# A mixture-of-experts stage on one core: batch entries grouped in blocks of 5 instead of 8, and half of the first weight matrix's split moved from VectorE to ScalarE

## The reference, cut to what matters

```python
for e in range(E):                       # E = 4
    h = gelu(context_c @ ew1[e] + eb1[e])          # 256 -> 1024
    y = h @ ew2[e] + eb2[e]                        # 1024 -> 256
    out = out + w_be[:, e] * mask[e] * y           # w_be is 0 where e is not one of the 2 picked
shared = gelu(context_c @ sw1 + sb1) @ sw2 + sb2
return out + shared
```

## Time and profile before

| What | Value |
|---|---|
| Median of three executions | 2313.76 us |
| Profiled execution: its own time / its span | 2309.97 us / 2308.2 us |
| TensorE matmul busy, share of the span | 2029.4 us (88%) |
| VectorE, ScalarE, GpSimd busy | 1332.8, 975.7, 359.8 us |
| Mean granted TensorE clock | 0.922 of full speed |
| Stretch of the routed units | 361.1 to 607.3 us from the start |

### The profile page before, as it was taken

One profiled execution on the slowest core, in us unless ns is written; L12 is line 12 of the kernel. 1 busy time (PEld: TensorE's weight loads), 2 busy tenths in 40 slices (PEclk: granted clock), 3 DMA queues, 4 the chain that ended last, 5 costly groups with the idle time before them and its releaser, 6 DMA issues. The chain is left out here.

```text
span 2308.2 us, 33746 instructions
## 1 busy us (share of the span) xinstructions
PE 2029.4 (88%) x13199; PEld 1629.9 (71%) x13199; DVE 1332.8 (58%) x2450; ACT 975.7 (42%) x1939; POOL 359.8 (16%) x276
## 2 busy tenths in 40 slices
PE   5699799999899999999999997489966867798798
PEld 3399788888677888888888786378953655456465
DVE  2577457778675446455464313565647457365796
ACT  2144445645453544544544322144433345454332
POOL 2258201323100000000000001057820000000000
PEclk7799899999999999999999998689987966899899
DMA  2555212232016022112000001445561002010000
GB/s 83 189 169 146 53 37 93 91 110 92 20 37 123 25 48 50 36 50 62 23 15 22 26 16 41 154 138 124 130 162 47 2 1 56 19 57 1 0 10 28
DMA packets 110104, 149.39 MB, mean 65 GB/s; under 512 B 6824, under 2 KB 92375, under 8 KB 109560
## 3 DMA queue, kind: packets, MB, share of 16 engines
q1 hardware_dynamic: 98780, 129.07, 19.2%
q0 software_dynamic: 11168, 18.18, 3.9%
HBM read 124.08 MB, written 23.15 MB: 64 GB/s over the span
## 5 line engine op out<-in xcount | busy, mean ns | idle before, releaser
L1828 DVE TENSOR_TENSOR m_h_lo<-m_hf,m_h_hi 128x512 fp32r<-128x512 f32 x256 | 173.7, 690 | 311.0 <-ACT m_hf L1803 307.2
L1800 ACT ACTIVATE m_h_hi<-m_h_ps,m_bT 128x512 fp32r<-128x512 f32 x256 | 177.0, 691 | 366.6 <-PE m_h_ps L396 346.8
L653 POOL DMA_INDIRECT token_sums<-e_y,slot_row x56 | 187.8, 3353 | 97.7 <-DVE e_y L779 83.6
L1803 ACT ACTIVATE m_hf<-m_h_ps,m_bT 128x512 f32<-128x512 f32 x256 | 175.0, 684 | 0.0
L738 ACT ACTIVATE e_h_hi<-e_h_ps,e_b1T 128x320 fp32r<-128x320 f32 (+1 forms) x128 | 78.0, 609 | 169.8 <-PE e_h_ps L396 113.8
L1481 DVE TENSOR_TENSOR c_h_lo<-c_hf,c_h_hi 128x512 fp32r<-128x512 f32 x120 | 91.9, 774 | 89.1 <-ACT c_hf L1431 88.4
L802 DVE TENSOR_TENSOR e_h_lo<-e_hf,e_h_hi 128x320 fp32r<-128x320 f32 (+1 forms) x128 | 72.3, 582 | 110.6 <-ACT e_hf L741 110.6
L1287 POOL TENSOR_TENSOR cT<-cT,c_yg 128x128 f32 x88 | 76.7, 872 | 269.2 <-DVE c_yg L1499 255.5
L1428 ACT ACTIVATE c_h_hi<-c_h_ps,c_b 128x512 fp32r<-128x512 f32 x88 | 62.2, 706 | 106.5 <-PE c_h_ps L396 105.9
L396 PE MATMUL m_y_ps<-m_h_hi,l_w_1hi 128*128 128x512 f32 x256 | 100.3, 392 | 3.4 <-issue 3.4
L396 PE MATMUL m_y_ps<-m_h_hi,l_w_0hi 128*128 128x512 f32 x256 | 99.7, 389 | 1.4 <-ACT m_gT L1814 1.4
(11 more groups left out here) (699 smaller groups left out, 5422.7 us busy)
## 6 DMA issues: line engine op xcount, KB each, us to landing
cT<-in_L_ffn_W_dram SPq DMA_DIRECT2D x30, 1024.0 KB, 5.3
res<-in_L_cond_ew_dram SPq DMA_DIRECT2D x22, 1024.0 KB, 5.1
cT<-in_L_ffn_w_dram SPq DMA_DIRECT2D x16, 1024.0 KB
res<-gates_rows SPq DMA_DIRECT2D x8, 1024.0 KB, 15.0
token_rows<-d_tok SPq DMA_DIRECT2D x2, 2112.0 KB, 10.4
token_sums<-res SPq DMA_DIRECT2D x2, 2048.0 KB, 7.9
res<-token_sums SPq DMA_DIRECT2D x8, 512.0 KB, 5.4
cT<-modulation_rows SPq DMA_DIRECT2D x8, 512.0 KB, 5.7
```

The lines of the kernel that those rows point to most:

```text
L653: pool.indirect_dma_start(out=sums, out_offset=bass.IndirectOffsetOnAxis(ap=st.slot_row[0:r, e, j:j + 1], axis=0), in_=y[0:r, e % 2, j, :] ...
L1800: act.activation(hs[0][:, f, :], h_ps[:, f % HB, :], ACT.Relu, bias=bT[:, at:at + 1])
L1803: act.activation(hf[:, f % HB, :], h_ps[:, f % HB, :], ACT.Relu, bias=bT[:, at:at + 1]).then_inc(act_done, 1)
L1828: dve.tensor_tensor(hs[1][:, f, :], hf[:, f % HB, :], hs[0][:, f, :].bitcast(F32), ALU.subtract).then_inc(h_ready, 1)
```

## The change

The block size `SLOTS` goes from 8 to 5 batch entries. The worst case is then (64 + 4 x 4) // 5 = 16 routed units, each 5 x 64 = 320 columns wide; the shared units keep their 512. So there are 20 units in all. All per-unit operations on `c_x`, `c_h`, `c_y`, `c_xg`, `c_yg` and `c_mix` become 320 wide in routed units, `take` runs for `f` = 0 to 4 alone, and GpSimd makes 5 additions per unit. The high part of W1 is no longer one cast on VectorE after `f` = 2 but two activations on ScalarE (`w1_high`, 1024 elements each), after its gelus of `f` = 1 and `f` = 2, ahead of `take`. VectorE's low halves of W1 wait for them. With 16 instead of 11 routed units the parity at the end changes, so the buffer pairs are swapped for the next phase.

```diff
-SLOTS = BLK // S
+SLOTS = 5
+WT = SLOTS * S
+MOST = (B + SLOTS - 1) // SLOTS
 ROUTED = (PICKED * B + E4 * (SLOTS - 1)) // SLOTS
...
+        wide = lambda u: BLK if u < NB else WT
...
-                        last = split_products(pe, h_ps[:, f % HB, :], [w[:, k, f * P:(f + 1) * P] for w in w1s[i % 2]],
-                                              [x[:, k, :] for x in xs[u % 2]], k == 0, k == KC - 1)
+                        last = split_products(pe, h_ps[:, f % HB, 0:wide(u)], [w[:, k, f * P:(f + 1) * P] for w in w1s[i % 2]],
+                                              [x[:, k, 0:wide(u)] for x in xs[u % 2]], k == 0, k == KC - 1)
...
             def take(u, s):
-                if u >= UNITS or u < NB:
+                if u >= UNITS or u < NB or s >= SLOTS:
                     return
...
+            def w1_high(i, c):
+                act.wait_ge(w1_in, 16 * i)
+                act.activation(w1s[i % 2][0][:, c, :], w1_raw[:, c, :], ACT.Copy).then_inc(w1_hi, 1)
+
...
+                    if u >= NB - 1 and f in (1, 2):
+                        w1_high(u - NB + 2, f - 1)
                     take(u + 1, f)
...
             def prepare(i, f):
-                if f == 2:
-                    dve.wait_ge(w1_in, 16 * i)
-                    dve.tensor_copy(w1s[i % 2][0][:, :, :], w1_raw).then_inc(w1_hi, 1)
                 if f in (3, 4):
-                    dve.wait_ge(w1_hi, i)
+                    dve.wait_ge(w1_hi, 2 * (i - 1) + f - 2)
                     w1_low(i, f - 3)
...
+        w1s, w2s = (pair if ROUTED % 2 == 1 else pair[::-1] for pair in (w1s, w2s))
```

More of the change, by code:

```diff
@@ L1207, in l1_cond_phase @@
         xs = [[sb(f"x_{i}{x}", [P, KC, BLK], F32R) for x in ("hi", "lo")] for i in range(2)]
-        xg = sb("xg", [P, KC, BLK])
+        xg = sb("xg", [P, KC, WT])
         hs = [sb(f"h_{x}", [P, FC, BLK], F32R) for x in ("hi", "lo")]
         hf = sb("hf", [P, HB, BLK])
-        yg, mix = sb("yg", [P, KC, BLK]), sb("mix", [P, SLOTS, S])
+        yg, mix = sb("yg", [P, KC, WT]), sb("mix", [P, SLOTS, S])
         bT, b1 = sb("bT", [P, (E4 + 1) * (FC + KC)]), [sb(f"b1_{i}", [P, FC]) for i in range(2)]
@@ L1223, in l1_cond_phase @@
         start = sb("start", [B, 1])
-        places, steps, nth = sb("places", [B, ROUTED * SLOTS]), sb("steps", [P, E4]), sb("nth", [P, ROUTED])
-        over, blocks, ends = sb("over", [P, E4, E4]), sb("blocks", [P, E4]), sb("ends", [P, E4])
+        places, steps, nth = sb("places", [B, ROUTED * SLOTS]), sb("steps", [P, MOST]), sb("nth", [P, ROUTED])
+        over, blocks, ends = sb("over", [P, E4, MOST]), sb("blocks", [P, E4]), sb("ends", [P, E4])
         past, owner = sb("past", [P, ROUTED, E4 - 1]), sb("owner", [P, ROUTED])
@@ L1267, in _ @@
                       allow_small_or_imprecise_dtypes=True).then_inc(const1, 1)
-            pool.iota(steps[:, :], pattern=[[SLOTS, E4]], base=0, channel_multiplier=0,
+            pool.iota(steps[:, :], pattern=[[SLOTS, MOST]], base=0, channel_multiplier=0,
                       allow_small_or_imprecise_dtypes=True).then_inc(const1, 1)
@@ L1328, in down @@
                     for c in range(KC):
-                        last = split_products(pe, y_ps[:, u % 2, c, :], [w[:, f, c * P:(c + 1) * P] for w in w2s[i % 2]],
-                                              [h[:, f, :] for h in hs], f == 0, f == FC - 1)
+                        last = split_products(pe, y_ps[:, u % 2, c, 0:wide(u)], [w[:, f, c * P:(c + 1) * P] for w in w2s[i % 2]],
+                                              [h[:, f, 0:wide(u)] for h in hs], f == 0, f == FC - 1)
                 last.then_inc(y_done, 1)
@@ L1412, in high @@
                     act.wait_ge(x_taken, (u - NB + 1) * SLOTS)
-                    act.activation(xs[u % 2][0][:, :, :], xg[:, :, :], ACT.Copy).then_inc(x_hi, 1)
+                    act.activation(xs[u % 2][0][:, :, 0:WT], xg[:, :, :], ACT.Copy).then_inc(x_hi, 1)
             def bias(u):
@@ L1427, in _ @@
                     act.wait_ge(up_done, n + 1)
-                    act.activation(hs[0][:, f, :], h_ps[:, f % HB, :], ACT.Gelu_apprx_tanh, bias=b[:, f:f + 1])
+                    act.activation(hs[0][:, f, 0:wide(u)], h_ps[:, f % HB, 0:wide(u)], ACT.Gelu_apprx_tanh, bias=b[:, f:f + 1])
                     if n >= HB:
                         act.wait_ge(h_ready, n - HB + 1)
-                    act.activation(hf[:, f % HB, :], h_ps[:, f % HB, :], ACT.Gelu_apprx_tanh, bias=b[:, f:f + 1]).then_inc(act_done, 1)
+                    act.activation(hf[:, f % HB, 0:wide(u)], h_ps[:, f % HB, 0:wide(u)], ACT.Gelu_apprx_tanh,
+                                   bias=b[:, f:f + 1]).then_inc(act_done, 1)
+                    if u >= NB - 1 and f in (1, 2):
+                        w1_high(u - NB + 2, f - 1)
                     take(u + 1, f)
@@ L1452, in x_low @@
                 x = y_ps[:, 0, :, :] if u == 0 else srcT[:, :, blk(u)] if u < NB else xg[:, :, :]
-                dve.tensor_tensor(xs[u % 2][1][:, :, :], x, xs[u % 2][0][:, :, :].bitcast(F32), ALU.subtract).then_inc(x_ready, 1)
+                n = wide(u)
+                dve.tensor_tensor(xs[u % 2][1][:, :, 0:n], x, xs[u % 2][0][:, :, 0:n].bitcast(F32), ALU.subtract).then_inc(x_ready, 1)
             def w1_low(i, c):
@@ L1480, in h_low @@
                 dve.wait_ge(act_done, n + 1)
-                dve.tensor_tensor(hs[1][:, f, :], hf[:, f % HB, :], hs[0][:, f, :].bitcast(F32), ALU.subtract).then_inc(h_ready, 1)
+                m = wide(u)
+                dve.tensor_tensor(hs[1][:, f, 0:m], hf[:, f % HB, 0:m], hs[0][:, f, 0:m].bitcast(F32), ALU.subtract).then_inc(h_ready, 1)
             def out_shared(u):
@@ L1498, in out_weighted @@
                 for c in range(KC):
-                    last = dve.scalar_tensor_tensor(out=yg[:, c, :], in0=y_ps[:, u % 2, c, :],
+                    last = dve.scalar_tensor_tensor(out=yg[:, c, :], in0=y_ps[:, u % 2, c, 0:WT],
                                                     scalar=bT[:, bass.ds(e * KC + (B2 + c), 1)],
@@ L1553, in keep_counts @@
                 dve.wait_ge(counted, 1)
-                link(dve.tensor_tensor(over[:, :, :], bc(ps[:, 0, 0:E4], 2, E4), bc(steps[:, :], 1, E4), ALU.is_gt))
+                link(dve.tensor_tensor(over[:, :, :], bc(ps[:, 0, 0:E4], 2, MOST), bc(steps[:, :], 1, E4), ALU.is_gt))
                 dve.tensor_copy(slot[:, :], ps[0:B, 0, E4:2 * E4]).then_inc(counts_kept, 1)
```

## The result

The changed kernel takes 2322.05 us in the median of 8 executions (2319.2 to 2333.14); the kernel before, measured with it, 2313.02. The ratio is 1.0046, with a 95% interval of 1.003 to 1.0062. A second, separate comparison gave 1.0048 (1.003 to 1.0067). So the change is slower by some 9 to 11 us. The forecast was 2330, inside 2314 to 2345.

What follows compares the result with a forecast made beforehand. TensorE was taken to bound the routed units at 21.76 us; after the change VectorE would, at 16.17. 15 x 16.17 + 20.24 less 0.4 gave 262.4 against 246.1, +16.3 us: median 2330, 8 in 10 within 2314 to 2345.

Steps and rivals of the forecast that it cites:

- TensorE alone: Routed units at 320 columns: 0.147 us a matmul, 14.1 us a unit, a 14 us gain if nothing else mattered.
- ScalarE: New routed unit: W1 copies of 0.97 us delay the gelus of f = 3, stalling TensorE about 0.95 us before group 7.
- VectorE: New routed unit: queue full from f = 3's delivery at 7.21 us, setting the period at 16.17 us.
- Collisions on the full queue: GpSimd additions beside VectorE's jobs in a routed unit: 1.5 collisions, 0.40 us a unit.
- Sum of the stretch: First routed matmul to GpSimd's last addition: 262.4 us against 246.1, 16.3 us more.
- the tail: Last routed unit, from its first matmul to the end of GpSimd's last addition: 20.24 us.
- The two holds: TensorE's two waits per routed unit: about 0.95 us for ScalarE before group 7, about 0.9 for the next input.
- rival A: Routed units: VectorE keeps up, only ScalarE's stall remains; period 15.25 us, stretch 248.4, +2 us, 2316; chance 0.16.
- What costs nothing: Weight loads, wider block-list comparison, the unit before the routed ones and swapped buffers: no added time; W1's load has 3.5 us cover.
- Rival D: TensorE's gaps lower the clock: 56 us more if a quarter of the matmuls ran at 1.2 GHz; chance 0.03.
- A collision's price: VectorE job beside a GpSimd addition: 0.27 us taken; an exclusive port lock could cost 0.45 us, period 16.45.
- The last step: Whole kernel: profiled execution from 2309.97 to 2326.3 us, median 3.8 us above the profiled one, so 2330.

Runs made afterwards that it cites:

- high34_x: Changed kernel with next input's low part before W2's last low half and ScalarE's two high halves behind f = 3 and 4: 2297.11 us, ratio 0.9925.
- x_early: Changed kernel with VectorE making the next input's low part before the last low half of W2: 2310.48 us, ratio 0.9985.
- high34: Changed kernel with ScalarE's two high halves behind f = 3 and 4, VectorE's order kept: 2314.3 us, ratio 1.0002.
- eight_act: Changed kernel with blocks of 8 again, W1's high part still on ScalarE: 2315.49 us, ratio 0.9996 to before.
- w2_first: Changed kernel with ScalarE's copies behind f = 5 and 6, VectorE splitting W2 first, loads swapped: 2314.51 us, ratio 1.0007.

## Why the prediction was right, point by point

- **TensorE alone.** 0.147 us a matmul: shown, 0.15 between starts. The floor of 14.1 us was reached within 0.3 in high34_x.
- **ScalarE.** `f` = 3 delivered at 7.21, measured 7.21. The copy's slot 0.97, measured 0.95. The stall before group 7 0.95, measured 1.0.
- **VectorE.** Five pairs of 1.54 and the input: the rows show them (401.32 to 402.86 is 1.54). Collisions on the full queue: 1.5 taken, about one measured, 0.33 us in all (399.45 to 401.32 is 1.87 instead of 1.54). Period 16.17, measured 16.11. One step was short: from `h_low` to `c_mix` I took 0.55 us, and the rows have 0.76 (394.45 to 395.21); it doesn't count here, since VectorE idles behind the scalings till `f` = 3.
- **Sum of the stretch.** +16.3, measured +15.0. Half of the difference is the period, the other half the tail: 20.24 forecast, 19.6 measured. The last unit has no `take` to do, three of them stand ahead of `f` = 3, and it is delivered 0.6 us earlier, which I left out. The two holds are the cause: taking away the one before the input (x_early) gives back 13.6 us, taking away ScalarE's (high34) 11.3, both (high34_x) 26.1. x_early also has the timing of my rival A: period 15.18 and stretch 247.5, where A had 15.25 and 248.4.
- **What costs nothing.** Nothing waited for the loads, and in eight_act, with blocks of 8, none of ScalarE's 1.94 us is seen.
- **The clock.** 1.00 in the whole routed stretch, with 31 gaps in it. Rival D is out, and so is what the rule of the Trainium skill ("TensorE: Matmul & The Clock Gate", section "A second HAM failure mode: psum-queue depth-cycling") would make of gaps of 1 us: no swing here.
- **A collision's price.** 0.27 us of VectorE on a full queue (1.48 for 1.21), 0.06 for the `c_h_lo` at 399.45 (0.54 for 0.48), and never the 0.45 us that I weighed against it. But the rows don't speak against a lock: GpSimd's addition is the one that waits when VectorE's job came first. The addition at 394.95 in w2_first takes 1.23 us for 0.45 and ends at 396.18, 0.32 us after the cast beside it (394.37 + 1.49 = 395.86).
- **What failed.** The last step: "so for the median I give 2330", which let the rest of the kernel stand still. The term was mis-sized: 16.3 forecast for the total, 9 to 10.5 measured. What differs are later stages, by up to 8 us in the attention piece with the granted clock there, and the one profile of before (246.7 there) did not show what its other two executions did. Why the usual execution of the changed kernel has the shorter one stays open. By the line of 0.5% the outcome is "the same", to which I gave 0.22, and not "slower", to which I gave 0.68; and 2322.05 lies 1 us below the 2323 at which my forecast's own range began.

## What to carry to other kernels

When units get shorter, don't compare sums of busy time: write down for one unit when each handover comes, in the written order of each engine, and find the job that the next unit waits for. Here one move of a job without urgency behind an urgent one, and one of two copies behind the point where four buffers cover them, turned +15 us of the stretch into -11 us. And a gain or loss early in a long kernel reaches the total only as far as the later stages let it; compare the stretch itself before explaining the total.

## What the runs showed of the hardware

Outside the changed stretch the executions of before differ in steps: 246.7 or 254.8 us in one piece, with a granted clock of 0.71 or 0.68 over it and 0.87 or 0.59 over the same 20 us of it, and 366.7 or 370.3 us at the end. An addition on GpSimd of 0.45 us costs VectorE 0.27 us when it falls on a full queue and nothing when VectorE is idle, so the same five additions cost 0.3 us a unit in one order and 1.35 in another. An addition that starts beside a VectorE job ends 0.32 us after that job: in w2_first one takes 0.67 us and one 1.23.
